# Third and sixth batch re-ordered around the attention state, ternary passes behind the last casts, twenty late normalise steps on GpSimd

## What is computed

```python
q = softmax(split(x @ Wq.T + bq), axis=-1)      # 16 heads of 16 channels
k = softmax(split(x @ Wk.T + bk), axis=-2)
v = split(x @ Wv.T + bv)
state = einsum('bhnd,bhne->bhde', k, v)
out = einsum('bhnd,bhde->bhne', q, state)
out = (out - mu) * rsqrt(var + EPS) * ln_g + ln_b
x = layernorm(x + out @ Wo.T + bo)
h = layer_norm(x, ln1_g, ln1_b) @ ternary_quant(w1).T + b1
h = layer_norm(gelu(h), ln2_g, ln2_b)
out = h @ ternary_quant(w2).T + b2
x = layernorm(x + out)
```

## Time and profile before

| | us |
|---|---|
| time, median of 3 runs | 551.71 (551.33 to 552.11) |
| profiled execution, device time | 551.79 |
| its span | 549.90 |
| TensorE busy | 532.1 (97%) |
| VectorE busy | 481.8 (88%) |
| ScalarE busy | 478.6 (87%) |
| GpSimd busy | 414.7 (75%) |

### The profile page before, as it was taken

The page is one execution under the profiler, slowest core; times in us unless marked ns, Lnnn a source line. Parts: engine busy times, 40 slices in busy tenths (PEclk is TensorE's granted clock), DMA queues, the critical chain, the costliest instruction groups (busy, mean ns, idle before and its releaser), DMA issues.

```text
span 549.9 us, 10913 instructions
## 1 busy us (share of the span) xinstructions
PE 532.1 (97%) x3541; PEld 492.0 (89%) x3541; DVE 481.8 (88%) x1227; ACT 478.6 (87%) x952; POOL 414.7 (75%) x429
## 2 busy tenths in 40 slices
PE   8999999999999999989999999999999999999993
PEld 7999999898999989879987999999999999999992
DVE  5888998989899898878788899999999999999896
ACT  5745789798978878778799999999999999999996
POOL 2965969877796986478468878888888877776782
PEclk9999999999999999999999999999999999999997
DMA  8530050320705021070011003322125253010012
GB/s 337 203 122 1 1 230 2 131 100 11 297 1 229 2 87 69 1 266 5 0 40 41 1 0 117 117 76 79 50 68 116 78 93 94 34 53 38 39 40 114
DMA packets 12679, 46.51 MB, mean 85 GB/s; under 512 B 1360, under 2 KB 3792, under 8 KB 10448
## 3 DMA queue, kind: packets, MB, share of 16 engines
q1 hardware_dynamic: 12336, 45.28, 23.7%
q10 hardware_dynamic: 288, 0.54, 0.3%
HBM read 29.01 MB, written 16.81 MB: 83 GB/s over the span
## 4 chain that ended last, share of the span: by engine, by line
PE 68%; ACT 11%; DVE 11%; POOL 5%; issue 3%; DMA 2%; SPq 0%; POOLq 0%; DVEq 0%; ACTq 0%
PE ring L2005 19%; PE qps_sps_aps_then_y L2027 19%; PE qps_sps_aps_then_y L1787 5%; PE qps_sps_aps_then_y L1893 5%; PE qps_sps_aps_then_y L1873 5%; PE ring L1815 5%; DVE z L1285 3%; PE ring L1945 2%; POOL xt_lo L462 2%; PE ring L1920 1%; PE ring L1908 1%; PE ring L1960 1%; ACT ek L745 1%; DMA xc<-in_x_first_dram 1%; POOL ff_accp_over_xt_lo L588 1%
## 5 line engine op out<-in xcount | busy, mean ns | idle before, releaser
L2027 PE MATMUL qps_sps_aps_then_y<-ff_w_over_xc_lo,ff_a_lo_over_qw 128*128 128x258 f32 x512 | 126.5, 283 | 0.0
L2027 PE MATMUL qps_sps_aps_then_y<-ff_w_over_xc_lo,ff_a_hi_over_xc_lo 128*128 128x258 f32 x512 | 126.4, 283 | 0.0
L1367 DVE SCALAR_TENSOR_TENSOR ff_a_lo_over_qw<-ring,ff_rho,ff_a_hi_over_xc_lo 128x512 fp32r<-128x512 f32 x128 | 92.8, 743 | 12.5 <-ACT ff_a_hi_over_xc_lo L881 11.4
L2005 PE MATMUL ring<-ff_ht_hi_over_qw,t 128*128 128x512 f32 x256 | 103.7, 405 | 0.1
L2005 PE MATMUL ring<-ff_ht_lo_over_xc_hi,t 128*128 128x512 f32 x256 | 100.5, 393 | 0.0
L2027 PEld LDWEIGHTS qps_sps_aps_then_y<-ff_w_over_xc_lo,ff_a_lo_over_qw 128*128 128x128 f32 x512 | 96.8, 189 | 3.3
L2027 PEld LDWEIGHTS qps_sps_aps_then_y<-ff_w_over_xc_lo,ff_a_hi_over_xc_lo 128*128 128x128 f32 x512 | 96.7, 189 | 3.4
L863 ACT ACTIVATE ring<-ring,bias 128x512 f32<-128x512 f32 x128 | 84.5, 689 | 6.7 <-PE ring L2005 5.5
L588 POOL TENSOR_TENSOR ff_accp_over_xt_lo<-ff_accp_over_xt_lo,ff_sq_over_ek_et_hi 128x512 f32<-128x512 f32 x66 | 86.0, 1303 | 2.0
L879 ACT ACTIVATE ff_sq_over_ek_et_hi<-ring 128x512 f32<-128x512 f32 x128 | 80.5, 629 | 0.5
L881 ACT CAST ff_a_hi_over_xc_lo<-ring 128x512 fp32r<-128x512 f32 x128 | 79.5, 621 | 0.0
(11 more groups left out here) (200 smaller groups left out, 1615.4 us busy)
## 6 DMA issues: line engine op xcount, KB each, us to landing
xt<-in_x_tok_dram SPq DMA_DIRECT2D x8, 1024.0 KB, 4.8
out_dram<-ff_z_over_et_lo SPq DMA_DIRECT2D x15, 512.0 KB, 2.7
x_scratch<-z SPq DMA_DIRECT2D x14, 514.0 KB, 3.6
ff_x_over_w_raw_xc<-x_scratch SPq DMA_DIRECT2D x14, 514.0 KB, 5.1
xc<-in_x_chan_dram SPq DMA_DIRECT2D x6, 1024.0 KB, 6.9
w_raw<-in_w_dram SPq DMA_DIRECT2D x2, 1024.0 KB, 5.4
ek<-in_x_chan_dram SPq DMA_DIRECT2D x1, 1024.0 KB, 8.2
x_scratch<-xt SPq DMA_DIRECT2D x2, 512.0 KB, 7.9
```

Source lines behind the costliest of these rows:

```text
L1367: nc.vector.scalar_tensor_tensor(out=ff_a_lo[:, m % DEPTH], in0=ff_bank(k, m), scalar=ff_rho[:, m:m + 1], in1=ff_a_hi[:, m % DEPTH].bitcas ...
L2005: mm = nc.tensor.matmul(ff_bank(k, m), t1[:, c, m * P:(m + 1) * P], h[:, k % 2, c], start=(c == 0 and j == 0), stop=(c == CH - 1 and j == 1))
L2027: last = nc.tensor.matmul(ff_yps[:, t, 0:C + 2], a[:, m % DEPTH, t * P:(t + 1) * P], ff_w2[:, m], start=(m == 0 and j == 0), stop=(m == FC ...
```

## The change

1. Batches 3 and 6 of the attention loop. VectorE does e_inverse and state(b-1) between residual(b-2,0) and residual(b-2,1), not behind both; ScalarE does state_out(b-1) ahead of squares(b-2,1).
2. ternary_out. Parts 0 and 1 move from between the et_high casts to behind product_out(b-1,6) and (b-1,7). Parts 2 and 3 of w1 move into batch 4, between projected_high(3) and normalise(2,1); parts 2 and 3 of w2 move to the last stage, behind state_out(6).
3. Last stage. projected_high(6) stands ahead of k_exponent(7,0); norm_rstd(5,1) on GpSimd stands behind both q_normalise(7).
4. normalise(5,1) and normalise(6,0) leave ScalarE. GpSimd now normalises 20 late tiles, three in each k from 4 to 10, where it had done 12, two in each k from 4 to 9.
5. The stores of the groups (5,1), (6,0), (6,1) go out at k = 6, 7, 8 and those of (7,0) and (7,1) both at k = 10; before it was k = 2, 3, 5, 7, 9.
6. squares(7,0) move from half-batch 0 to 1 and squares(7,1) from 1 to 2, each with its norm_rstd on GpSimd.

```diff
--- before.py
+++ after.py
@@ -360,10 +360,10 @@
             def store(b, g):
                 if not 0 <= b < NB:
                     return
-                if (b, g) <= (NB - 2, 0):
+                if (b, g) <= (NB - 3, 0):
                     sp.wait_ge(x1_ok, T * b + GROUP * (g + 1))
                 else:
-                    sp.wait_ge(x1_late, GROUP * (NG * (b - NB + 2) + g))
+                    sp.wait_ge(x1_late, GROUP * (NG * (b - NB + 3) + g))
                 gs = slice(g * GROUP, (g + 1) * GROUP)
                 if b < NB - 1:
                     sp.dma_start(x1_scratch[b, :, gs], z[:, z_slot(b, g)]).then_inc(x1_out[z_slot(b, g)], 16)
@@ -415,15 +415,14 @@
             for k in range(1, NK):
                 if k >= 2:
                     ff_store(k - 2)
-                if k == 2:
+                if k == 6:
                     store(NB - 3, 1)
-                elif k == 3:
+                elif k == 7:
                     store(NB - 2, 0)
-                elif k == 5:
+                elif k == 8:
                     store(NB - 2, 1)
-                elif k == 7:
+                elif k == 10:
                     store(NB - 1, 0)
-                elif k == 9:
                     store(NB - 1, 1)
                 if k + XB < NK:
                     ff_load_over(k + XB)
@@ -514,9 +513,10 @@
                 var = last_var[:, gs] if b == NB - 1 else z[:, z_slot(b, g), :, C]
                 nc.gpsimd.tensor_tensor(var, vaZ[:, gs], eps[:, gs], ALU.add).then_inc(z_fin, 1)
 
-            def late_normalise(b, ts):
-                pool.wait_ge(z_fin, 4 * (NG * b + ts[-1] // GROUP + 1))
-                for t in ts:
+            def late_normalise(first, last):
+                for n in range(first, last):
+                    b, t = divmod(T * (NB - 3) + GROUP + n, T)
+                    pool.wait_ge(z_fin, 4 * (NG * b + t // GROUP + 1))
                     row = z_tile(b, t)
                     nc.gpsimd.tensor_scalar(row, row, rsZ[:, b % RZ, t:t + 1], nmr[:, b % RZ, t:t + 1], ALU.mult, ALU.add
                                             ).then_inc(x1_late, 1)
@@ -626,9 +626,9 @@
                 if b in (2, 5):
                     ternary_round(b // 5, 2)
             norm_rstd(NB - 3, 0)
-            norm_rstd(NB - 3, 1)
             q_normalise(NB - 1, 0)
             q_normalise(NB - 1, 1)
+            norm_rstd(NB - 3, 1)
             tok_lo(NB - 1, 0)
             tok_lo(NB - 1, 1)
             ff_norm_rstd(0)
@@ -645,7 +645,6 @@
             ff_keep_residual(0, 1)
             ff_square_sum(0, 1)
             attention_rstd(NB - 1, 1)
-            norm_rstd(NB - 1, 0)
             ff_square_sum(0, 2)
             ff_square_sum(0, 3)
             ff_square_sum(0, 4)
@@ -659,7 +658,7 @@
             ff_hidden_rstd(0)
             ff_square_sum(1, 3)
             ff_square_sum(1, 4)
-            norm_rstd(NB - 1, 1)
+            norm_rstd(NB - 1, 0)
             ff_square_sum(1, 5)
             ff_norm_rstd(4)
             ff_keep_residual(2, 0)
@@ -669,6 +668,7 @@
             ff_square_sum(2, 2)
             ff_hidden_rstd(1)
             ff_square_sum(2, 3)
+            norm_rstd(NB - 1, 1)
             for k in range(4, NK + 1):
                 ff_square_sum(k - 2, 4)
                 ff_out_rstd(k - 4)
@@ -681,10 +681,8 @@
                 ff_square_sum(k - 1, 2)
                 ff_hidden_rstd(k - 2)
                 ff_square_sum(k - 1, 3)
-                if k in (4, 5):
-                    late_normalise(NB - 2, (2 * k - 4, 2 * k - 3))
-                elif k in (6, 7, 8, 9):
-                    late_normalise(NB - 1, (2 * k - 12, 2 * k - 11))
+                if 4 <= k <= 10:
+                    late_normalise(3 * (k - 4), min(3 * (k - 3), T * 2 + GROUP))
             ff_square_sum(NK - 1, 4)
             ff_out_rstd(NK - 3)
             for m in range(5, FC):
@@ -933,10 +931,17 @@
                 state_copy(b - 1)
                 squares(b - 2, 0)
                 q_bias(b + 1, 1)
-                squares(b - 2, 1)
-                state_out(b - 1)
+                if b in (3, 6):
+                    state_out(b - 1)
+                    squares(b - 2, 1)
+                else:
+                    squares(b - 2, 1)
+                    state_out(b - 1)
                 normalise(b - 2, 0)
                 projected_high(b - 1)
+                if b == 4:
+                    ternary_out(0, 2)
+                    ternary_out(0, 3)
                 normalise(b - 2, 1)
                 k_exponent(b, 0)
                 chan_hi(b + 2)
@@ -960,11 +965,7 @@
                     ternary_top(b // 6, 3)
                 q_exponent(b + 1, 1)
                 et_high(b, 0)
-                if b in (3, 6):
-                    ternary_out(b // 6, 0)
                 et_high(b, 1)
-                if b in (3, 6):
-                    ternary_out(b // 6, 1)
                 product_out(b - 1, 5)
                 pt_high(b, 2)
                 pt_high(b, 3)
@@ -972,24 +973,25 @@
                 et_high(b, 3)
                 if b in (2, 5):
                     ternary_bottom(b // 5, 0)
+                product_out(b - 1, 6)
+                product_out(b - 1, 7)
                 if b in (3, 6):
+                    ternary_out(b // 6, 0)
+                    ternary_out(b // 6, 1)
                     ternary_bottom(b // 6, 2)
                     ternary_bottom(b // 6, 3)
-                product_out(b - 1, 6)
-                product_out(b - 1, 7)
                 if b in (1, 4):
                     absolute_sums(b // 4)
                 if b in (2, 5):
                     ternary_bottom(b // 5, 1)
-                if b in (3, 6):
-                    ternary_out(b // 6, 2)
-                    ternary_out(b // 6, 3)
             state_copy(NB - 2)
             squares(NB - 3, 0)
             state_out(NB - 2)
+            ternary_out(1, 2)
+            ternary_out(1, 3)
             squares(NB - 3, 1)
+            projected_high(NB - 2)
             k_exponent(NB - 1, 0)
-            projected_high(NB - 2)
             normalise(NB - 3, 0)
             k_exponent(NB - 1, 1)
             product_out(NB - 2, 0)
@@ -1043,7 +1045,6 @@
             ff_gelu(0, 4)
             ff_square_and_high(0, 3)
             ff_square_and_high(0, 4)
-            squares(NB - 1, 0)
             ff_gelu(0, 5)
             ff_gelu(0, 6)
             ff_square_and_high(0, 5)
@@ -1057,9 +1058,8 @@
             ff_ht_high(2, 0)
             ff_gelu(1, 2)
             ff_square_and_high(1, 2)
-            squares(NB - 1, 1)
+            squares(NB - 1, 0)
             ff_ht_high(2, 1)
-            normalise(NB - 3, 1)
             ff_gelu(1, 3)
             ff_gelu(1, 4)
             ff_square_and_high(1, 3)
@@ -1077,7 +1077,7 @@
             ff_ht_high(3, 0)
             ff_gelu(2, 2)
             ff_square_and_high(2, 2)
-            normalise(NB - 2, 0)
+            squares(NB - 1, 1)
             ff_ht_high(3, 1)
             ff_gelu(2, 3)
             ff_gelu(2, 4)
@@ -1532,9 +1532,14 @@
             q_denominator(1, 1)
             for b in range(1, NB - 1):
                 residual(b - 2, 0)
-                residual(b - 2, 1)
-                e_inverse(b - 1)
-                state(b - 1)
+                if b in (3, 6):
+                    e_inverse(b - 1)
+                    state(b - 1)
+                    residual(b - 2, 1)
+                else:
+                    residual(b - 2, 1)
+                    e_inverse(b - 1)
+                    state(b - 1)
                 if b in (2, 5):
                     ternary_scales(b // 5)
                 q_inverse(b, 0)
```

## The result

The changed kernel takes 561.70 us in the median (559.83 to 564.07, four runs), beside 551.91 us (551.33 to 552.19, four runs) for the kernel before. The ratio is 1.0182, with a 95% interval of 1.0165 to 1.0199. The forecast was 552.0 with a range of 549.5 to 554.3, so it was wrong, and on the slow side. The profiled execution took 564.07 us, the slowest of the four; its span is 562.2, 12.3 more than that of before. What follows is read from it, so it explains some 2.4 us more than the median has.

A forecast was written before the change was run, and what follows sets the result against it. TensorE, busy 97% of the span, was taken as the bound, leaving only its waits to win. Terms 0.0 (batches 3 and 4), +0.7, -0.1, -0.3, -0.2, -0.4 made -0.3 (gains positive): median 552.0 us, range 549.5 to 554.3.

The forecast's parts named there:

- Batch 3, state before residual.: Batch 3: earlier r_f removes state_transpose's 0.9 wait, later k_exponent makes TensorE wait again; net -0.2 (gains positive).
- Ternary passes.: Batches 3 and 4: state_sum(3,0) wait goes, +0.9; batch 4's exponent gives 0.7 back; with the reorder 0.0 together.
- third rival: Batch 4: passes cost their whole 1.24, chain no earlier: 552.7; chance 0.24 together with the milder store rival.
- Batch 6.: Batch 6: state_sum(6,0) wait of 0.9 goes, 0.2 more at q_transposes(6,0); +0.7, bounds +0.3 and +1.2.
- Last stage.: Last stage: 1.0 at q_transposes goes, returns at state_sum(7,0), k_exponent(7,1) chain unmoved; -0.1, bounds -0.3 and +0.5.
- Half-batch 0.: First FFN half-batch: GpSimd sums delay residual(7,1), -1.7; waits behind it go, +1.4; taken -0.3, bounds -1.0 and +1.6.
- Half-batch 2: Half-batch 2: norm_rstd(7,1) ahead of sums makes VectorE's total late, -0.2; third late tile from k = 4 to 10: 0.
- Stores.: Load 14: two stores at k = 10, load lands at 477, ff_var 0.9 late, half within slack; -0.4, bounds 0 and -2.2.
- the milder rival: Load 14: slower stores, load landing 478.5, gives 553.8; chance 0.24 together with the third rival.
- The second: Load 14: stores and load run one after another, ff_var waits 8 us: 559; chance 0.05 in full.

The follow-up runs named there:

- The kernel with the waiting sums: Changed kernel with one wait more: GpSimd's four sums of half-batch 0 wait until residual(7,1) has ended on VectorE; 555.89 us, 1.0074 against the kernel before.
- the sums early: Kernel before with only GpSimd's norm_rstd(7,0) moved behind the third of half-batch 0's four sums, ScalarE untouched; 554.62 us beside 551.83, ratio 1.0044.

## Why the prediction was wrong, point by point

- **Batch 3, state before residual.** The early r_f, the squares at 105.9 and the exponent on time were right (the exponent ended at 113.80, 0.03 later than before). The step that failed is "normalise, projected_high and k_exponent follow", taken as the whole list of those that wait for squares(1,1). norm_rstd and q_normalise on GpSimd, 1.5 later, were not in it, and so not their overlap with r_lo. The term was -0.2 for each of the two batches; measured alone they made -2.5 together. With q_normalise ahead of norm_rstd r_lo was free and the loss stayed at 2.7, over norm_rstd, normalise and the exponent, so this second chain had less room than the prediction gave it.
- **Ternary passes.** Both waits at state_sum went, and the pair in batch 4 took the first gain back at q_transposes(4,0), as forecast. How much it took was wrong: ScalarE's chain came 0.1 earlier and not 0.7, the exponent ended at 146.91 (forecast 146.25, third rival 146.95), and behind batch 4 the shift was +0.7 with the moves alone. Without the reorder's part the forecast was 0.2 + 0.9 = 1.1, and the medians gave 1.1; since batch 4 cost more than forecast and the profile shows 0.3, that agreement is partly luck.
- **Batch 6.** The term was +0.7. With the reorder in it batch 6 lost 0.7 (1.75 to 2.4), by the same r_lo.
- **Last stage.** Term -0.1, measured -1.05. "k_exponent(7,1) waits for its own input already, so nothing in this chain moves" failed: its input is made by VectorE behind r_lo, r_lo took 1.5 longer, and the exponent came 1.1 later.
- **Half-batch 0.** The mechanism was named, GpSimd's sums over VectorE's work in this place, but not the steps that it met, and its size was wrong: -0.3 against some -3.7 with the clock. The step that failed is the list of VectorE's work beside the sums. I counted residual(7,1) alone, because it has two SBUF inputs, and passed over znm and ff_norm_apply, which have one. They took 1.32 and 3.18 instead of 0.17 and 1.14, and made everything behind them 3.2 late. So residual(7,1) didn't meet the sums at all; one of its four steps was held up (1.50), by ff_keep_residual. The lower clock behind the wait, 1.4 us, was not in the sum at all.
- **Half-batch 2** cost 0.4 where 0.2 was forecast, and the third tile nothing that can be seen.
- **Stores.** Alone the landing was about as forecast (476.4 for 477), and the loss of 0.9 was not: the term was -0.4. ff_var was late by 0.6, about what slack there was (0.5), and was then held for 1.0 more by GpSimd's next sum, an overlap that the sum of the prediction left out. In the changed kernel the load came 2.0 later by its DMAs, the milder rival's case, and with the same 1.0 on top TensorE came 3.05 later where that rival had 2.2; the clock added 1.55. Why stores and load took 2.0 us more there is open. The kernel with the waiting sums has the same order and didn't show it, so it may be that one execution's.
- **The rivals.** The second, at load 14, came in its milder form, and the third held for batch 4; none held the loss of the reorder or of the last stage. Each slow case was one mechanism, and several came at once: -2.5 for the reorder, -1.05 for the last stage, some -3.7 for half-batch 0 and up to -4.6 for load 14 with its clock. How they add is known to about 1 us only: by the shifts between 100 and 260 us the attention part loses 3.7 in the changed kernel, and its three groups of edits alone 3.4 - 0.55 + 1.25 = 4.1; by the medians the three make 2.5 - 1.1 + 1.05 = 2.45.

The Trainium skill ("SBUF — State Buffer", section "Who interferes with whom") says that `tensor_scalar`, too, can enter a mode in which VectorE uses the port pair that GpSimd also reads through, and that whoever issues first holds it for its whole instruction. The trace agrees on both: L1352 and L1290, `tensor_scalar` steps with one SBUF input, took 3.18 and 1.32 under the sums instead of 1.14 and 0.17, and in the reorder with q_normalise ahead it was GpSimd's step of 0.20 that took 0.96 under VectorE's r_lo. I had quoted the half of this rule about two inputs and left out the other half, which speaks of the step that decided here.

## What to carry to other kernels

When an instruction on one engine is made later or earlier, list everything on VectorE and GpSimd whose time window moves with it, and look for pairs of SBUF-to-SBUF work that come to lie over one another; such a pair cost 1 to 2 us here, as much as the waits being removed. Short steps count too: one of 0.17 took 1.32 under a sum of GpSimd. A wait that only holds GpSimd's sums back until VectorE is through was worth 5.8 us in the changed kernel, so an idle GpSimd beside a busy VectorE can be the better plan. And put the clock into the sum: behind waits of TensorE of 1.6 to 2.9 us it fell in some places and not in others, and each fall set TensorE back by 1.4 to 1.6 us beside the wait, of which later waits took some back.

## What the runs showed of the hardware

- r_lo (VectorE, 128x768, two SBUF inputs) takes 0.95 us alone and 2.47 to 2.62 under q_normalise of GpSimd (1.94), in each of the changed kernel's three places and in the kernels with the reorder and the last stage alone.
- Four `tensor_scalar` steps of 128x256, fp32, from SBUF to SBUF take 1.14 us alone and 3.18 under GpSimd's sums of 1.3 to 1.4; one of 128x4 takes 0.17 and 1.32. A `scalar_tensor_tensor` of 128x4 with two SBUF inputs (ff_var) takes 0.16 and, under one such sum, 1.18 to 1.20. ff_a_lo (L1367), which reads one of its inputs from PSUM, took 1.40 for two under the same sums, as it does alone.
- TensorE's clock stayed at 1.00 behind waits of 2.0 us (two, in the reorder with q_normalise ahead) and of 1.62 at attend in the last stage of the changed kernel. It was at its lower level behind a wait of 1.63 at the same attend in the kernel with the last stage alone, behind waits of 2.1 (twice in the kernel with the squares alone, once with the sums early), behind 2.09 and 1.88 close together, and behind 2.85. So the length of the wait alone didn't tell whether it fell. Each fall set TensorE back by 1.4 to 1.6 us by the shifts.
- How much of a fall stays at the end varies. With the sums early, the one run of five with a mean clock of 0.997 took 554.02 and the four with 0.992 or 0.993 took 553.82 to 554.73. In the reorder with q_normalise ahead, the one with 0.992 took 555.98 and the three with 0.995 took 554.43 to 554.63. The changed kernel's two faster runs have mean clocks of 0.992 and 0.993 and its two slower ones 0.989, which fits one more fall; but the four runs with the squares alone all have 0.989 and spread by 2.2 us, so the clock needn't be all of it. It was not tried apart.
- The load behind a store of 512 KB that runs beside an output store alone was issued 6.8 us after the store; behind two of them, 9.3 to 9.6 after the first.
